# Macaron block: order of the q/k/v stage, its convolutions, gate groups, norms and head sums

## The reference

```python
def _short_conv_1d(x, weight):                 # 4 taps along the sequence, one filter per feature
    xp = jnp.pad(x, ((0, 0), (K - 1, 0), (0, 0)))
    shifts = jnp.stack([xp[:, i:i + x.shape[1], :] for i in range(K)], axis=-1)
    return jnp.sum(shifts * weight[None, None, :, :], axis=-1)
...
x = _layernorm(x)
q = silu(_short_conv_1d(x @ Wq + bq, q_conv)).reshape(B, S, h, d); q = q / (norm(q) + 1e-06)
k = silu(_short_conv_1d(x @ Wk + bk, k_conv)).reshape(B, S, h, d); k = k / (norm(k) + 1e-06)
v = silu(_short_conv_1d(x @ Wv + bv, v_conv)).reshape(B, S, h, d)
alpha = sigmoid(x @ Wa + ba); beta = sigmoid(x @ Wb + bb)      # one rate per token and head
out_gate = silu(x @ Wg + bg)
...
# recurrence over the sequence with q, k, v, alpha, beta; group norm; (out_gate * y) @ Wo + bo
```

## Time and profile before

| | us |
|---|---|
| median of 3 runs (lowest, highest) | 3531.27 (3527.9, 3531.66) |
| the profiled execution | 3538.78 |
| its span, first to last instruction | 3536.9 |
| q/k/v stage in it | 608.5 to 1632.2 |
| busy in that stage: PE, DVE, ACT, POOL | 929.8, 816.3, 712.8, 594.9 |

### The profile page before, as it was taken

How to read it: one execution, slowest core, us unless ns; L and a number is a source line. 1 busy time by engine, 2 the same in 40 slices (tenths; PEclk the granted TensorE clock), 3 DMA queues, 4 the chain that set the end, 5 groups by cost and what they waited for, 6 DMA issues and landing times. The chain is left out here.

```text
span 3536.9 us, 191423 instructions
## 1 busy us (share of the span) xinstructions
PE 3288.2 (93%) x83236; PEld 2760.8 (78%) x83236; DVE 2753.6 (78%) x4491; ACT 1583.4 (45%) x2344; POOL 1823.7 (52%) x1707
## 2 busy tenths in 40 slices
PE   7999998799999999995999999999996987999999
PEld 5888886576767767674999999999995765888887
DVE  6767775787888878784899999999997856676765
ACT  4455553577777777772112211221113433545454
POOL 1232322566555665654777888888874431223232
PEclk8999999899999999997999999999998998999999
DMA  3122212232323323225777777777774772212121
GB/s 119 71 97 81 101 77 95 74 99 82 103 73 92 93 74 99 86 76 133 187 198 199 200 199 199 203 201 197 200 197 149 228 221 99 107 71 107 71 107 59
DMA packets 486525, 452.84 MB, mean 128 GB/s; under 512 B 55488, under 2 KB 448832, under 8 KB 467264
## 3 DMA queue, kind: packets, MB, share of 16 engines
q1 hardware_dynamic: 484160, 449.56, 42.0%
q10 hardware_dynamic: 2304, 2.49, 0.3%
HBM read 331.33 MB, written 120.60 MB: 128 GB/s over the span
## 5 line engine op out<-in xcount | busy, mean ns | idle before, releaser
L350 POOL TENSOR_TENSOR ffn_out<-ffn_gate,ffn_xres 128x512 f32<-128x512 f32 x128 | 182.1, 1451 | 784.2 <-DVE ffn_gate L254 783.8
L784 DVE SCALAR_TENSOR_TENSOR ain_conv<-ain_padded,ain_taps,ain_conv 128x512 f32<-128x512 f32 x384 | 416.5, 1085 | 13.8 <-DVE ain_tail L781 0.3
L1464 ACT ACTIVATE rec_u<-rec_ps_end 128x256 f32<-128x256 f32 x128 | 49.2, 384 | 631.0 <-PE rec_ps_end L1516 631.0
L885 POOL TENSOR_TENSOR ain_conv<-ain_conv,ain_term 128x512 f32<-128x512 f32 x192 | 272.3, 1418 | 16.0
L1232 POOL TENSOR_TENSOR rec_d_norm<-rec_dmat,rec_early 128x512 f32<-128x512 f32 x128 | 162.7, 1271 | 174.8 <-DVE rec_dmat L1314 174.8
L940 ACT ACTIVATE ain_buf<-ain_conv 128x512 f32<-128x512 f32 x192 | 121.0, 630 | 232.3 <-POOL ain_conv L885 146.7
L46 PE MATMUL ffn_ring<-ffn_mixkh,ffn_wkh 128*128 128x512 f32 x512 | 218.4, 427 | 6.5 <-DVE ffn_mixkl L196 6.5
L46 PE MATMUL ffn_ring<-ffn_mixrh,ffn_wrh 128*128 128x512 f32 x512 | 215.4, 421 | 9.2 <-DVE ffn_mixrl L306 9.2
L46 PE MATMUL ffn_ring<-ffn_mixkh,ffn_wkl 128*128 128x512 f32 x512 | 203.2, 397 | 0.0
L46 PE MATMUL ffn_ring<-ffn_mixrh,ffn_wrl 128*128 128x512 f32 x512 | 202.0, 395 | 0.0
L46 PE MATMUL ffn_ring<-ffn_act_h,ffn_wvh 128*128 128x512 f32 x512 | 201.8, 394 | 0.0
(11 more groups left out here) (249 smaller groups left out, 10285.6 us busy)
## 6 DMA issues: line engine op xcount, KB each, us to landing
rec_early<-coeffs SPq DMA_DIRECT2D x512, 128.0 KB, 3.0
streams<-ain_buf SPq DMA_DIRECT2D x48, 1024.0 KB, 5.1
rec_qkv<-streams SPq DMA_DIRECT2D x126, 384.0 KB, 3.3
rec_qk_pe<-streams SPq DMA_DIRECT2D x127, 256.0 KB, 3.4
rec_late<-coeffs SPq DMA_DIRECT2D x504, 64.0 KB, 2.3
ffn_xres<-in_x SPq DMA_DIRECT2D x16, 1024.0 KB
ain_x<-x SPq DMA_DIRECT2D x16, 1024.0 KB, 4.9
gate<-ain_gate SPq DMA_DIRECT2D x16, 1024.0 KB, 6.7
```

Of the source, the lines that this page charges most:

```text
L350: added = nc.gpsimd.tensor_tensor(out[:, m, :], gate[:, m, :], xres[:, m, :], ALU.add)
L784: nc.vector.scalar_tensor_tensor(out=out[:], in0=pad[:, n:n + TOK], scalar=taps[:, u // KT, u % KT, n:n + 1], in1=out[:], op0=ALU.mult, op ...
L885: nc.gpsimd.tensor_tensor(out[:], out[:], term[:], ALU.add).then_inc(pool_conv, 1)
L1464: nc.scalar.activation(u[:], ps_end[:, :, 1, :], ACT.Copy).then_inc(u_ready, 1)
```

## The change

All twelve convolutions run on VectorE, in the order of the units; GpSimd keeps the weights' low parts and the sums of squares. The ring has three banks for the units and one for the gate; a gate group stands behind every third unit on TensorE and its activation at the same place on ScalarE. The root of the norms, the norms and their stores of tile t move into the slot of tile t+1. The square of tile t+2 stands at the end of slot t on ScalarE, its centring on VectorE between the convolutions 10 and 11 of slot t; the variance of tile t+1 stands behind unit 1 on TensorE, its mean is made in the slot before. The head sums are made in two groups of four matmuls, each with 32 columns of weights into its own quarter of the partitions. The rates and coefficients lie in those quarters, so one sigmoid and full passes over 128 partitions serve alpha and beta, and each coefficient is stored in four stores of four rows. The diff, cut:

```diff
+        UNITS = 3 * KT
+        CONV_STEPS = TAPS + 1
+        NORM_DMAS, DECAY_DMAS = 16 * 5 * KT, 16 * 2 * KT
+        HEADS_0, BIASED_0 = 1, 3
...
-            for n in range(2):
...
-            for n in "kvg":
+            for r in range(3):
+                for m in range(KT):
+                    at, head = m * HD + r * HG, r // 2 * H + m * HG
+                    sp.dma_start(ab_bias[at:at + HG, :], ab_bias_dram[head:head + HG, :]).then_inc(ab_loaded, 16)
+            for n in "gkv":
...
+            def store_rows(pair, s, k, tile, first, done):
+
+                for m in range(KT):
+                    at = m * HD + first * HG
+                    sp.dma_start(coeffs[bass.ds(pair, 1), s % 2 * CPT:(s % 2 + 1) * CPT, k, s // 2, m:H:KT, :].rearrange("a c h i -> h (a c) i"),
+                                 tile[at:at + HG, :].rearrange("h (c i) -> h c i", i=CH)).then_inc(done, 16)
+
+            def store_norms(pair, s):
+                t = pair * 4 + s
+                sp.wait_ge(norm_ready, t + 1)
+                store_rows(pair, s, K_QNORM, inv_norm, Q_ROWS, norm_stored)
+                store_rows(pair, s, K_KNORM, inv_norm, K_ROWS, norm_stored)
+                sp.wait_ge(gamma_scaled, t + 1)
+                store_rows(pair, s, K_QDECAY, gamma_norm, Q_ROWS, norm_stored)
+                store_rows(pair, s, K_KDECAY, gamma_norm, K_ROWS, norm_stored)
+                store_rows(pair, s, K_BETA, gamma_norm, B_ROWS, norm_stored)
+
...
-                    sp.wait_ge(silued, 12 * t + 4 * j + 4)
+                    sp.wait_ge(silued, UNITS * t + 4 * j + 4)
                     store_stream(t, j)
+                    if j == 0 and not first:
+                        store_norms(pair - (s == 0), (s - 1) % 4)
                     if j == 1:
                         sp.wait_ge(ends_ready, t + 1)
-                        store_rows(pair, s, K_DECAY, decay, 2 * H)
-                        sp.dma_start(last_decay.rearrange("h g n -> (h g) n")[:, bass.ds(t * CPT, CPT)],
-                                     gamma_end[2 * H:3 * H, :]).then_inc(coeff_stored, 16)
+                        store_rows(pair, s, K_DECAY, decay, Q_ROWS, decay_stored)
+                        for m in range(KT):
+                            sp.dma_start(last_decay[:, m, bass.ds(t * CPT, CPT)], gamma_end[m * HD:m * HD + HG, :]).then_inc(decay_stored, 16)
                 sp.wait_ge(gate_ready, KT * t + 2 * KT)
                 sp.dma_start(gate_dram[bass.ds(t, 1), :, :, :].rearrange("a p k n -> (a p) k n"), gate[:]).then_inc(gate_stored, 16)
-                sp.wait_ge(norm_ready, t + 1)
-                store_rows(pair, s, K_QNORM, inv_norm, 2 * H)
...
-                sp.wait_ge(gamma_scaled, t + 1)
-                store_rows(pair, s, K_QDECAY, gamma_norm, 2 * H)
-                store_rows(pair, s, K_KDECAY, gamma_norm, 3 * H)
 
...
             def centre(t):
+                if not isinstance(t, int) or t > 0:
+                    dve.wait_ge(x_low, t)
                 dve.wait_ge(mean_done, t + 1)
                 nc.vector.tensor_tensor(xc[:], x[:], ps_mean[:].unsqueeze(1).to_broadcast([P, KT, TOK]),
                                         ALU.subtract).then_inc(centred, 1)
 
-            def deviations(t):
+            def variances(t):
                 dve.wait_ge(var_done, t + 1)
                 nc.vector.tensor_scalar_add(var_tok[:], ps_mean[:, 0:KT], LN_EPS).then_inc(var_copied, 1)
+
+            def deviations(t):
                 dve.wait_ge(std_ready, t + 1)
                 nc.vector.reciprocal(rstd_tok[:], std_tok[:]).then_inc(inverted, 1)
                 dve.wait_ge(inverted, t + 1)
...
-            def slot(t, s, ahead):
+                nc.vector.tensor_tensor(gamma_norm[:], gamma[:], inv_norm[:], ALU.mult).then_inc(gamma_scaled, 1)
+
+            def slot(t, s, ahead=2, first=False):
                 mask_tails(t)
+                for u in range(3):
+                    convolve(t, u)
                 if ahead:
-                    centre(t + 1)
-                for u in (0, 1, 3, 4):
-                    convolve(t, u)
-                decays(t)
+                    variances(t + 1)
+                convolve(t, 3)
+                if ahead:
+                    deviations(t + 1)
+                if not first:
+                    norms(t - 1)
+                convolve(t, 4)
                 if ahead == 2:
                     sums(t + 2)
-                convolve(t, 6)
-                if ahead:
-                    deviations(t + 1)
-                convolve(t, 7)
+                convolve(t, 5)
                 if ahead:
                     normalise(t + 1)
-                convolve(t, 9)
+                convolve(t, 6)
+                convolve(t, 7)
+                decays(t)
+                convolve(t, 8)
                 if ahead:
                     low(t + 1, 1 - s)
+                convolve(t, 9)
                 convolve(t, 10)
-                norms(t)
+                if ahead == 2:
+                    centre(t + 2)
+                convolve(t, 11)
 
             sums(0)
             weight_high("q")
...
+            choose_rows()
+            slot(0, 0, first=True)
+            with dve.Fori(0, NT // 2 - 2) as r:
+                slot(2 * r + 1, 1)
+                slot(2 * r + 2, 0)
+            slot(NT - 3, 1)
+            slot(NT - 2, 0, ahead=1)
+            slot(NT - 1, 1, ahead=0)
+            norms(NT - 1)
...
-            def slot(t, more):
-                pool.wait_ge(tails_masked, t + 1)
...
-                for u in (2, 5, 8, 11):
-                    convolve(t, u)
+                nc.gpsimd.tensor_tensor(sum2, half2[:, 0, :], half2[:, 1, :], ALU.add).then_inc(summed2, 1)
 
...
+            def gates(t, m):
+                if m == 0:
+                    act.wait_ge(gate_stored, 16 * t)
+                    act.wait_ge(w_split["g"], 1)
+                act.wait_ge(group_done, 16 * t + 4 * m + 4)
+                nc.scalar.activation(gate[:, m, :], ring[3][:], ACT.Silu, bias=bias[:, 3, m:m + 1]).then_inc(gate_ready, 1)
+
+            def decay_rates(t):
+                act.wait_ge(ab_done, t + 1)
+                nc.scalar.activation(alpha_beta[:], ps_ab[:], ACT.Sigmoid, bias=ab_bias[:]).then_inc(ab_ready, 1)
+
+            def head_norms(t):
+                act.wait_ge(heads_summed, HEADS_0 + 2 * t + 2)
+                act.wait_ge(norm_stored, NORM_DMAS * t)
+                nc.scalar.activation(inv_norm[:], ps_rows[:], ACT.Sqrt).then_inc(rooted, 1)
+
+            def slot(t, s, ahead=2, first=False):
+                for u in range(UNITS):
                     shift(t, u)
                     if u > 1:
-                        silu(t, u - 2, more)
+                        silu(t, u - 2, ahead)
+                    if u % 3 == 2:
+                        gates(t, u // 3)
                     if u == 4:
-                        act.wait_ge(ab_done, t + 1)
-                        act.wait_ge(coeff_stored, COEFF_DMAS * t)
-                        nc.scalar.activation(alpha[HROWS, :], ps_ab[HROWS, :], ACT.Sigmoid,
-                                             bias=ab_bias[HROWS, :]).then_inc(alpha_ready, 1)
-                        nc.scalar.activation(beta[HROWS, :], ps_ab[BROWS, :], ACT.Sigmoid,
-                                             bias=ab_bias[BROWS, :]).then_inc(beta_ready, 1)
-                    if more and u == 7:
-                        deviation(t + 1)
-                    if more and u == 10:
+                        decay_rates(t)
+                        if ahead:
+                            deviation(t + 1)
+                        if not first:
+                            head_norms(t - 1)
+                    if ahead and u == 8:
                         high(t + 1, 1 - s)
-                act.wait_ge(heads_summed, 8 * t + 8)
-                nc.scalar.activation(inv_norm[HROWS, :], ps_rows[HROWS, :], ACT.Sqrt).then_inc(rooted, 1)
-                silu(t, 10, more)
-                act.wait_ge(gate_stored, 16 * t)
-                act.wait_ge(w_split["g"], 1)
-                for m in range(KT):
-                    if m == 2:
-                        silu(t, 11, more)
-                    act.wait_ge(group_done, 16 * t + 12 + m + 1)
-                    nc.scalar.activation(gate[:, m, :], ring[m][:], ACT.Silu, bias=bias[:, 3, m:m + 1]).then_inc(gate_ready, 1)
+                silu(t, 10, ahead)
+                silu(t, 11, ahead)
+                if ahead == 2:
+                    act.wait_ge(heads_summed, HEADS_0 + 2 * t + 1)
+                    square(t + 2)
 
...
+            square(1)
+            slot(0, 0, first=True)
+            with act.Fori(0, NT // 2 - 2) as r:
+                slot(2 * r + 1, 1)
+                slot(2 * r + 2, 0)
+            slot(NT - 3, 1)
+            slot(NT - 2, 0, ahead=1)
+            slot(NT - 1, 1, ahead=0)
+            head_norms(NT - 1)
...
-            def head_sums(t, n):
```

(53 more changed lines are left out.)

208 lines of the change are left out of this document (82 added, 126 removed).

## The result

The changed kernel took 3573.74 us (median of 4 runs, 3570.62 to 3579.2) against 3531.47 us for the kernel before (4 runs, 3527.9 to 3538.45). The ratio is 1.0122, 95% interval 1.0109 to 1.0134: slower by 42.3 us. The forecast was 3584 us and slower by 52.7 us.

A forecast was written before the change was run, and what follows sets the result against it. A cross-engine loop of waits in the q/k/v stage was taken to bind: 6.4 + 12.4 + 6.1 + 38.8 = 63.7 us, plus 1.4 us clock loss, 65.1 us a tile; +52.7 us in all gives 3584 us, range 3535 to 3618.

The forecast's parts named there:

- The loop: q/k/v stage: round of waits from one tile's convolution 11 to the next's, 63.7 us at full pace, 65.1 with clock loss.
- Steps (1) and (3): (1) silu(11), square, GpSimd sums: 6.4 us; (3) ScalarE from shift(4) through sigmoid and root: 6.1 us.
- Step (2): TensorE in the loop: variance matmuls, then unit 2, gate group, units 3 and 4: 12.4 us.
- Step (5): TensorE's clock drops after 6 us idle in every tile: 1.4 to 2.7 us a tile, 1.4 taken.
- Step (4): VectorE in the loop: reciprocal, diagonal, norms, eight convolutions, decays and sums, three passes: 38.8 us.
- Head sums: Two groups of four 32-column matmuls on TensorE: cost between two and eight old ones, both ends free under the idle.
- Stores: SP's queue: 28 small stores a tile instead of seven, 0.64 us an issue; twenty stand alone at the stage's end.
- Rival (D): SP's queue becomes late, gate stores hold back gates(0) and the loop: 9 us more a tile, 3710 us; chance 0.05.
- (C): The loop holds but TensorE's clock does too: 14 x 1.4 us less, 3564 us; chance 0.20.
- (B): TensorE stays the bound and gets shorter, loop under about 60 us: at 56 us a tile 3471 us; chance 0.13.

The follow-up runs named there:

- var3: Changed kernel with TensorE's variance product of tile t+1 behind unit 3 instead of unit 1: 3488.0 us.
- sqearly: Changed kernel with ScalarE's square of tile t+2 ahead of the silu of unit 11 instead of behind it: 3521.4 us.
- rootonly: Changed kernel with ScalarE's roots (next tile's deviation and head norms) in front of the sigmoid instead of behind it: 3553.9 us.
- fill: Changed kernel plus twenty unread 128-column matmuls on TensorE between unit 1 and the variance product: 3554.4 us.
- poolconv: Changed kernel with every third convolution (units 2, 5, 8, 11) back on GpSimd: 3633.3 us.
- wide: Changed kernel with the head sums as eight products with 128-wide weights instead of 32 columns on column tiles: 3578.1 us.
- hs6wide: hs6 with the head sums as eight products with 128-wide weights: 3527.2 us.
- best2: var3 plus second head sum behind unit 11, roots in front of the sigmoid, and earlier centring and square of tile t+2: 3467.9 us.
- hs6: var3 plus second head sum behind unit 11 instead of 10, and the 1/sigma spread matmul behind unit 6 instead of before it: 3464.8 us.
- hs7r: hs6 plus roots in front of the sigmoid on ScalarE, and the first head sum behind unit 7 instead of unit 6: 3427.2 us.

## Why the prediction was right

**The loop** was the right one. The trace shows it whole, and three runs confirm it from three sides: three products fewer in it (var3), the square off its end (sqearly), the sigmoid out of its middle (rootonly), each with a time that falls. Forecast 65.1 us a tile, measured 64.97. That the two agree to 0.1 us is luck, since two errors of about 1 us a tile, some 14 us each in all, cancel:
- Steps (1) and (3): 6.4 and 6.1 us forecast, 6.3 and 6.1 measured.
- Step (2), the variance and four products at full pace, was right: fill has 0.8 us and 2.9 us for the first two. Step (5), the clock, was mis-sized: 1.4 us taken, 2.6 us measured (variance 1.73 against 0.8, unit 2 4.57 against 2.9), at my upper bound of 2.7. Those are the numbers of the tile shown; over the tiles 1 to 14 the loss was 2.4 us on average. The idle time was 5.5 us against 6 forecast. I had taken the row whose idle time was nearest to mine; the other row was the better one. One third of the loss, 0.9 us, is in the variance matmuls, which stand first behind the wait; I had only thought of products.
- Step (4), VectorE: 38.8 forecast, 37.8 measured. The norms take 4.45 us instead of 4.8 (their addition 0.42 where the earlier trace rows has 0.81), sums and decays 4.7 instead of 5.0, and three long passes 6.6 instead of 6.9. The rows that I took stood in a stage in which GpSimd was convolving; now it is idle there. poolconv bears this out: beside the convolving GpSimd the first pass of the decays took 1.75 us (at 1101.58), in the changed kernel 0.68.

**Head sums.** Both ends cost nothing, as the prediction said; wide shows the dear end (4.3 us, not told apart from zero), the trace the cheap one. The point at which the cover goes was shown by hs6wide: +62 us.

**Stores.** 0.64 us an issue forecast, 0.37 measured, 5.4 us less in the tail: the largest miss that no other made good, and the reason why the last tile took 69.1 us from its start to the last issue and not 74.7. The stage, from SP's first issue to its last, grew by 45.0 us (1020.9 to 1065.9) against 52.7. Rival (D) did not come up: gate stores landed 7.9 us after issue instead of 6.7, and no gate activation of the stage stands among ScalarE's waits for a DMA.

**Rivals.** (C), the clock holds, is out by the windows above; fill comes nearest to what it would have given, 3554.4 us against my 3564. (B) was wrong for this order of instructions, but var3 shows that it was only two units away: 58.75 us a tile, with TensorE idle for 4.1 of them, as soon as the variance matmul stands where its sums are ready.

**Medians and profiled runs.** From one profiled execution to the other the difference is 31.8 us, though the stage grew by 45.0 and its start by 1.5. The missing 14.7 us lie in stages that the change doesn't touch: the recurrence took 1055.2 us instead of 1061.3, the output stage 223.9 instead of 230.6, the last ffn 610.8 instead of 612.8. In the profiles of the twelve experiments these stages vary by as much (recurrence 1054.9 to 1059.9, output 222.4 to 231.0), and the recurrence of the kernel before is the longest of all. So this looks like the spread between executions (the one of before lay 7.3 us above its median, the other 3.1 below); what causes it is not shown.

## What to carry to other kernels

When an instruction is moved to an earlier place in an in-order queue, write down the round that it closes, from its producer back to itself one tile later, across all engines, and compare its length with the busiest engine: here no engine was busy for more than 56 us a tile (TensorE 726.29 us in the 13 tiles of 844.55) and the round had 65. The cure was not less work but a later place for one small matmul. And once a wait is removed, add up the next engine's own work before naming the gain; best2, hs6 and hs7r missed what I had expected of them because a wait moved on, or another engine's round was as long, when one wait had gone. Where TensorE stands, price what follows at the lower clock too: it was 2.4 us a tile here, 2.8 in poolconv.

## What the runs showed of the hardware

- Four matmuls of 512 columns with 128x32 F32 weights, each to its own 32 rows of PSUM, took 1.00 us together, little more than one old head sum of 128x128 (0.86 us up to the next F32 matmul); with 128-wide weights four took 3.0 us. The Trainium skill, TensorEngine Tiling (Array Packing), Theoretical Speedup, gives up to four times the speed for a small dimension of at most 32; the trace has three times. The drain on a change of mode, under Key Properties there, is at most 0.1 us on the way back, by which the next product was longer; on the way in it is inside the 1.00 us.
- After 5.5 us of idle the granted clock was 0.50 for some 5 us after the work began again, and 2.6 us were lost. Shorter waits did it too, and not always: in var3's tile at 1052.78, behind 2.6 us, the group took 1.87 us and the next product 4.87 instead of 2.9; behind the same 2.6 us unit 11 was slow in 3 of 14 tiles of the changed kernel and, with the group, in 13 of 14 of poolconv; behind 2.1 us the first group of hs6wide was slow in 12 of 14.
- Twenty matmuls that nobody reads made the kernel 19 us faster.
- A small store (8 KB, four rows) in a long row of its kind was issued in 0.37 us, a little over half of what the bias loads of before took the earlier trace rows.
